# Moving a router's transposes, logits and row split into the last batch of the layer before it, and merging two blocks of an MoE layer

## The chip, the cores and the metric

The kernel runs on one core of one Trainium2 chip. The metric is device time in microseconds, the median of several executions. The core has five engines with instruction queues of their own: TensorE (PE; its weight loads are listed apart as PEld), VectorE (DVE), ScalarE (ACT), GpSimd (POOL) and SyncE (SP, which only issues transfers here). They meet by semaphores. TensorE's clock has two levels, 1.2 and 2.4 GHz, and the profile gives the granted share of the full one.

## The reference

One decoder layer on x of 32 batches x 112 rows x 256 columns, in float32. Three parts, each followed by a residual and a layer norm.

1. Self part: a linear attention with 16 heads and a feed-forward with gelu.
2. Cross attention: 16 heads of 64 over a context of 375 rows per batch. Per batch: normalise x and the context, q, k and v projections, softmax, values, output projection, then `x = layernorm(x + out)`.
3. A mixture of 8 experts, two per row, with 17 places (CAP) per expert and batch:

```
probs = softmax(x @ Wr + br);  topk_p, topk_e = top_k(probs, 2)
pos   = place of each row in its expert's queue, within the batch (cumulative count)
keep  = pos < 17
buf   = rows of x scattered to (expert, batch, pos)      # dispatch
y     = relu(buf @ W1 + b1) @ W2 + b2                    # per expert
out   = sum over the two choices of y[its place] * p * keep
x     = layernorm(x + out)
```

## The kernel before, in words

x stays in SBUF as `x_sb` (112 x 32 x 256, float32) through all three layers. Products that need accuracy are done in three float16 products of high and low halves (`split_product`, L62 to L64). Every stage is a block: each engine runs its own program, and all engines meet at the end of a block.

**Layer 2, the cross attention (L758 to L1439).** One batch is 16 steps (heads) s. In step s of batch b TensorE does, in this order: `turn_scores` (three transposes of the softmax's row block, L1016), one piece of the q, k or v projection of batch b+1 (L62 to L64), in even steps the scores of heads s+4 and s+5 (`scores`, L1007) and the values of heads s-2 and s-1 (`values`, L1032), and in step 3 the output projection of the batch before (`out_rows`). ScalarE does the exp of head s+2 (L1122), then the high half of the turned block (`turned_high`, L1128), then the high half of the piece. VectorE does the low halves, the reciprocal of the sum (L1236) and the masked maximum of head s+4 (`mask_max`, L1231). GpSimd normalises head s+2 (L1393) and prepares batch b+2. The scores of the next two heads wait until both maxima of the last two are taken. In the last batch, b = 31, there is no next batch: the pieces are gone and only turn, scores, values and the output projections are left. Its output rows are ready with the layer norm of batch 31 (`norm_out`, L1262). The projections' results go through three PSUM banks `pb` in turn. TensorE's program for the 32 batches is written out; on ScalarE, VectorE, GpSimd and SyncE batches 0, 1, 30 and 31 are written out, and 2 to 29 are a hardware loop of 14 turns over two batches.

**Route (L1503 to L1678).** After layer 2's block: for 8 groups of four batches, VectorE copies x to `xs` (L1631), TensorE turns it (8 float32 transposes, L1586), ScalarE copies the turned block to `xt` (L1604) and writes x's high half `x_hi` (L1606), TensorE multiplies it with the 256 x 8 router weights (8 float32 matmuls with 8 moving columns, L1577), VectorE adds the bias (L1621) and writes x's low half (L1627). `x_hi` and `x_lo` lie in `y_t`, which the experts fill later. Then the choice of two experts: 17 dependent VectorE operations on 112 x 256 (L1656 to L1678), with one exp on ScalarE and one counting matmul on TensorE. The split of the first expert's weights `w1` (high on ScalarE L1487, low on VectorE L1492) lies within route; the low half of `w2` comes first in the experts' block.

**Dispatch (L1681 to L1748).** A block of its own: per group, VectorE builds `gather` (0/1 matrix of 112 x 136 per batch, L1726), TensorE multiplies x_hi and x_lo with it (4 matmuls a batch into 4 + 4 banks, L1745), ScalarE copies the high result to `buf_hi` (L1711), VectorE the low result to `buf_lo` (L1721).

**Experts and combine.** The experts' block begins when dispatch has ended, and TensorE's first matmul there waits for `w1`'s low half.

Of the kernel before, what the change touches and what calls it, by code (L numbers as in the profile page):

```python
# [20 lines left out]
P = 128  # L21
# [5 lines left out]
KD = D // P  # L27
# [39 lines left out]
def decoder_kernel(nc, a, out):  # L67
    root = ExitStack()
    with root:
# [17 lines left out]
        layer2(nc, a, x_sb, ident, half_neg, passed, sb_in, psum_in, sem)  # L87
        layer3(nc, a, out, x_sb, ident, half_neg, passed, sb_in, psum_in, sem)
# [669 lines left out]
def layer2(nc, a, x_sb, ident, half_neg, passed, sb_in, psum_in, sem):  # L758
# [6 lines left out]
    with stack:  # L765
# [6 lines left out]
        stage = [sb(f"b_stage{i}", [P, WCOLS], F32) for i in range(NST)]  # L772
# [34 lines left out]
        o_hi, o_lo = (sb(f"b_o_{n}", [P, KI, T], F16) for n in ("hi", "lo"))  # L807
        z = sb("b_z", [T, D], F32)
# [25 lines left out]
        PRE = (turns(0) + [("P", 0, s) for s in range(PREP_AT)] + turns(1) + [("P", 0, s) for s in range(PREP_AT, NCH)])  # L834

        def body_uses(b):

            uses = []
            for s in range(H):
                if not is_last(b):  # L840
                    uses.append(("P", s))
                if s == W_AT and not is_first(b):
                    uses.append(("W", 0))
                if has_prep(b):
                    uses += [(kind, at.index(s)) for kind, at in (("X", X_AT), ("C", C_AT)) if s in at]
            if is_last(b):
                uses.append(("W", 1))
            return uses

        def is_first(b):  # L850
            return isinstance(b, int) and b == 0

        def is_last(b):
            return isinstance(b, int) and b == B - 1

        def has_prep(b):
            return not isinstance(b, int) or b + 2 < B

        PER = len(body_uses(None))
        assert PER % NPB == 0  # L860

        def use_in(b, item):

            less = 0 if is_first(b) else PER - len(body_uses(0))
            if is_last(b):
                less += PER - len(body_uses(B - 2))
            return b, len(PRE) - less + body_uses(b).index(item)

        def use_piece(n, s):
            return (0, PRE.index(("P", 0, s))) if is_first(n) else use_in(n - 1, ("P", s))  # L870

        def use_turn(n, kind, k):
            return (0, PRE.index((kind, n, k))) if isinstance(n, int) and n < 2 else use_in(n - 2, (kind, k))

        def use_out(b):
            return use_in(b, ("W", 1)) if is_last(b) else use_in(b + 1, ("W", 0))

        def ready(use):
            return use[0] * PER + use[1] + 1

        def freed(use):
            return use[0] * (PER // NPB) + use[1] // NPB + 1

        def bank(use):
            return pb[use[1] % NPB]

        def free_of(use):
            return pb_free[use[1] % NPB]

        w_loaded = [sem(f"b_w_loaded{i}") for i in range(NST)]  # L890
        w_hi_done, w_lo_done, vec_loaded = sem("b_w_hi_done"), sem("b_w_lo_done"), sem("b_vec_loaded")
        ctx_loaded = [sem(f"b_ctx_loaded{i}") for i in range(2)]
# [18 lines left out]
        def x_row(b):  # L911
            return x_sb[:, bass.ds(b, 1), :].rearrange("p a d -> p (a d)")

        def batches(eng, body):

            body(0, 0)
            body(1, 1)
            with eng.Fori(1, B // 2 - 1) as i:
# [8 lines left out]
        def _(sp):  # L927
            def load(n, par):
                settle(sp, passed, (xc_done, n - 1))
                sp.dma_start(ctx[:, par, :, :], a["ctx_1024"][bass.ds(n, 1), :, :].rearrange(  # L930
                    "a (p t) d -> p (a t) d", t=JT)).then_inc(ctx_loaded[par], 16)
                settle(sp, passed, (mask_done, n - 1))
                sp.dma_start(mask8[:, par, :], a["mask_BxS2_bf1"][bass.ds(n, 1), :].rearrange(
                    "a s -> (a s)").partition_broadcast(T)).then_inc(mask_loaded[par], 16)
# [5 lines left out]
            for i, src in enumerate(weights.values()):  # L940
                at_least(sp, w_lo_done, i - NST + 1)
                sp.dma_start(stage[i % NST][:, :].rearrange("p (k n) -> p k n", n=src.shape[2]), src).then_inc(w_loaded[i % NST], 16)
                if i == 0:
                    load(1, 1)
            with sp.Fori(1, B // 2) as i:
                for par in range(2):
                    load(2 * i + par, par)

        @block.tensor
        def _(pe):  # L950
            def claim(use):
                at_least(pe, pb_free[use[1] % NPB], freed(use) - 1)
                return bank(use)
# [37 lines left out]
            def written(n, *pieces):  # L991

                last = {}
                for s in sorted(PIECES.index(piece) for piece in pieces):
                    use = use_piece(n, s)
                    last[use[1] % NPB] = use
# [49 lines left out]

            def body(b, par):
                for s in range(H):
                    turn_scores(b, s)
                    if not is_last(b):  # L1050
                        piece(b + 1, 1 - par, s)
                    if s % 2 == 0 and s + AHEAD < H:
# [30 lines left out]
            for b in range(B):  # L1083
                body(b, b % 2)
# [4 lines left out]
        def _(act):  # L1089
# [28 lines left out]

            def softmax_exp(b, h):
# [17 lines left out]
            def split_high(name):  # L1137
                i = list(weights).index(name)
                act.wait_ge(w_loaded[i % NST], 16 * (i // NST + 1))
                act.activation(hi[name][:, :], stage[i % NST][:, :], ACT.Identity, scale=WSCALE).then_inc(w_hi_done, 1)  # L1140

            def body(b, par):
                for s in range(H):
# [9 lines left out]
                    if not is_last(b):  # L1153
                        piece_high(b + 1, 1 - par, s)
                    if s == SPLIT_O_AT and is_first(b):
# [24 lines left out]
            batches(act, body)  # L1180
# [3 lines left out]
        def _(dve):  # L1184
            def prep_stats(n, par, tiles):
                dve.wait_ge(ctx_loaded[par], 16 * (half_of(n) + 1))
# [20 lines left out]
            def piece_low(n, par, s):  # L1207
# [15 lines left out]
                ins.then_inc(pb_free[use[1] % NPB], 1)  # L1223

            def mask_max(b, par, h):

                waits = [(s_ready, H * b + h + 1), (p_exp, H * b + h - 1)]
                if h == 0:
# [3 lines left out]
                                         ALU.add, ALU.min, neg_max[:, h % 4:h % 4 + 1]).then_inc(s_masked, 1)  # L1232

# [30 lines left out]
            def split_low(name):  # L1264
                i = list(weights).index(name)
                dve.wait_ge(w_hi_done, i + 1)
                dve.scalar_tensor_tensor(lo[name][:, :], stage[i % NST][:, :], WSCALE, hi[name][:, :], ALU.mult,  # L1267
                                         ALU.subtract).then_inc(w_lo_done, 1)

            def body(b, par):  # L1270
                for s in range(H):
# [6 lines left out]
                    elif s == 0 and not is_first(b):  # L1278
                        piece_low(b, par, NCH - 1)
                    turned_low(b, s)  # L1280
# [25 lines left out]
            def half_of(n):  # L1306

                return n // 2 if isinstance(n, int) else halves[0]

            halves = [None]  # L1310
# [18 lines left out]
            body(0, 0)  # L1329
            body(1, 1)  # L1330
            with dve.Fori(1, B // 2 - 1) as i:
                halves[0] = i + 1
                for par in range(2):
                    body(2 * i + par, par)
            body(B - 2, 0)
            body(B - 1, 1)
# [6 lines left out]
        def _(pool):  # L1343
            def mask(n, par):
                settle(pool, passed, (mask_loaded[par], 16 * (half_of(n) + 1)),
# [32 lines left out]
            def split_ctx(n, par, k):  # L1378
                use = use_turn(n, "C", k)
                settle(pool, passed, (pb_free[use[1] % NPB], freed(use)))  # L1380
# [14 lines left out]

            def body(b, par):
                for s in range(H):
                    if s + 2 < H:
                        normalise(b, s + 2)
                    elif not is_last(b):  # L1400
                        normalise(b + 1, s + 2 - H)
                    if s == 0 and not is_last(b):
# [13 lines left out]
            def half_of(n):  # L1416
                return n // 2 if isinstance(n, int) else halves[par_of[0]]

            halves, par_of = [None, None], [0]
# [10 lines left out]
            body(0, 0)  # L1430
            body(1, 1)
            with pool.Fori(1, B // 2 - 1) as i:
                halves[0], halves[1] = i + 1, i
                for par in range(2):
                    par_of[0] = 1 - par
# [653 lines left out]
```

## Time and profile before

| | us |
|---|---|
| median of 3 runs | 2368.42 (2366.4 to 2376.06) |
| the profiled execution: its own time | 2368.95 |
| the profiled execution: span of its instructions | 2367.0 |
| TensorE busy | 2215.9 (94%) |
| VectorE busy | 1552.4 (66%) |
| ScalarE busy | 1385.2 (59%) |
| GpSimd busy | 744.0 (31%) |

TensorE's mean granted clock is 0.964. The page also cuts the span into 40 equal slices and gives busy shares in tenths; this is TensorE's row and the row of its clock:

```profile
PE   5999999999996599999999999999999999779998
PEclk8999999999998799999999999999999999659999
```

A slice is 59.2 us. Slices 13 and 14 hold the change from layer 1 to layer 2; slices 35 and 36 (2012 to 2130 us) hold the last batch of layer 2, route and dispatch. The last four slices are experts and combine.

### The profile page before, as it was taken

Reading aid. Unit: us, or ns where it says so; the run is one execution under the profiler, and the core shown is the slowest. Engines: PE = TensorE matmul, PEld = TensorE weight load, DVE = VectorE, ACT = ScalarE, POOL = GpSimd, SP = SyncE. Lnnn points to the kernel's source line nnn. Section 1 sums busy time; section 2 is a strip of 40 time slices with the busy share of each in tenths; the row PEclk is TensorE's granted clock in tenths of the full one; section 3 lists DMA queues with packets and bytes.
Section 4 is the critical chain, followed back from the end, with each engine's and each line's share of the span. In section 5 each row is a group of like instructions: output and inputs, shape, how many; then the busy total and the mean of one; then the engine's idle time right before and its main releaser. Section 6 shows DMA issues by size and latency. Waiting matters only on the chain. (4 is left out here: it accounts for less than half of the span.)

```text
span 2367.0 us, 60858 instructions
## 1 busy us (share of the span) xinstructions
PE 2215.9 (94%) x20706; PEld 1659.8 (70%) x20706; DVE 1552.4 (66%) x4402; ACT 1385.2 (59%) x3136; POOL 744.0 (31%) x1303
## 2 busy tenths in 40 slices
PE   5999999999996599999999999999999999779998
PEld 4776876876875367776767677777767676668886
DVE  4545545545544478777777777787777777466657
ACT  5556446446441467677676767676776767444444
POOL 1121221211211344444454544444444544100003
PEclk8999999999998799999999999999999999659999
DMA  5100000000000300000000000000000000212302
GB/s 137 36 2 1 0 0 0 0 0 0 0 1 1 100 11 14 15 9 15 9 15 10 15 9 15 12 13 15 9 15 9 15 2 2 73 22 87 106 1 63
DMA packets 45672, 50.94 MB, mean 22 GB/s; under 512 B 19120, under 2 KB 37664, under 8 KB 45504
## 3 DMA queue, kind: packets, MB, share of 16 engines
q1 hardware_dynamic: 45504, 48.45, 6.9%
q8 instruction: 136, 2.23, 0.4%
q14 instruction: 32, 0.26, 0.0%
HBM read 44.78 MB, written 3.67 MB: 20 GB/s over the span
## 5 line engine op out<-in xcount | busy, mean ns | idle before, releaser
L1393 POOL TENSOR_SCALAR p_norm<-p,p_rec 112x375 f32<-112x375 f32 x512 | 303.2, 593 | 638.2 <-DVE p_rec L1236 575.1
L1240 DVE TENSOR_TENSOR pt_lo<-b_t,pt_hi 125x336 f16<-125x336 f32 x512 | 258.0, 504 | 149.0 <-ACT pt_hi L1128 143.9
L1231 DVE CUSTOM_DVE_ANT_0 s_neg<-b_s,mask_bias 112x375 f32<-112x375 f32 x512 | 274.8, 537 | 94.0 <-PE b_s L1007 89.3
L1128 ACT ACTIVATE pt_hi<-b_t 125x336 f16<-125x336 f32 x512 | 227.3, 444 | 145.1 <-PE b_t L1016 141.3
L1122 ACT ACTIVATE p<-s_neg,neg_max 112x375 f32<-112x375 f32 x512 | 308.1, 602 | 1.3 <-DVE neg_max L1231 1.3
L1016 PE MATMUL b_t<-ident,p_norm 112*125 112x112 f32 x1536 | 274.6, 289 | 10.7 <-POOL p_norm L1393 5.4
L1016 PEld LDWEIGHTS b_t<-ident,p_norm 112*125 112x125 f32 x1536 | 216.1, 191 | 51.8 <-POOL p_norm L1393 28.9
L646 POOL TENSOR_SCALAR_AFFINE_SELECT sm<-sm 112x448 f32<-112x448 f32 x128 | 71.5, 581 | 433.1 <-ACT sm L430 433.1
L1116 ACT ACTIVATE v_hi<-b_pb 125x512 f16<-125x512 f32 x192 | 114.8, 598 | 111.3 <-PE b_pb L64 111.1
L62 PE MATMUL b_pb<-cn_hi,b_wk_hi 128*128 128x375 f16 x512 | 165.9, 324 | 1.9 <-DVE b_wk_lo L1267 1.9
L64 PE MATMUL b_pb<-cn_hi,b_wk_lo 128*128 128x375 f16 x512 | 165.1, 322 | 0.0
L63 PE MATMUL b_pb<-cn_lo,b_wk_hi 128*128 128x375 f16 x512 | 164.9, 322 | 0.0
L1113 ACT ACTIVATE k_hi<-b_pb 128x375 f16<-128x375 f32 x256 | 124.2, 485 | 61.3 <-PE b_pb L64 56.7
L430 ACT ACTIVATE sm<-a_s 112x448 f32<-112x448 f32 x128 | 62.5, 540 | 163.2 <-PE a_s L299 163.2
L62 PE MATMUL b_pb<-b_wv_hi,cn_hi 128*125 128x512 f16 x384 | 147.6, 384 | 5.3 <-issue 3.8
L64 PE MATMUL b_pb<-b_wv_hi,cn_lo 128*125 128x512 f16 x384 | 147.2, 383 | 0.0
L63 PE MATMUL b_pb<-b_wv_lo,cn_hi 128*125 128x512 f16 x384 | 147.0, 383 | 0.0
L1221 DVE SCALAR_TENSOR_TENSOR v_lo<-b_pb,v_hi 125x512 f16<-125x512 f32 x192 | 131.0, 682 | 18.2 <-ACT v_hi L1116 18.2
L1032 PE MATMUL b_o<-pt_hi,v_hi 125*64 125x112 f16 x1536 | 139.0, 223 | 1.8 <-DVE pt_lo L1240 1.8
L1216 DVE SCALAR_TENSOR_TENSOR k_lo<-b_pb,k_hi 128x375 f16<-128x375 f32 x256 | 138.3, 541 | 2.0 <-ACT k_hi L1113 2.0
L1032 PEld LDWEIGHTS b_o<-pt_hi,v_hi 125*64 125x64 f16 x1536 | 87.2, 110 | 73.0 <-issue 43.5
L1032 PE MATMUL b_o<-pt_lo,v_hi 125*64 125x112 f16 x1536 | 133.0, 215 | 0.0
(246 smaller groups left out, 6460.4 us busy)
## 6 DMA issues: line engine op xcount, KB each, us to landing
w_raw<-in_L_ffn_W_dram SPq DMA_DIRECT2D x16, 1024.0 KB, 7.4
ctx<-in_ctx_dram SPq DMA_DIRECT2D x32, 375.0 KB
out_dram<-c_z SPq DMA_DIRECT2D x8, 448.0 KB, 3.2
x_sb<-in_x_dram SPq DMA_DIRECT2D x1, 3136.0 KB, 19.1
ff<-in_L_attn_w_dram SPq DMA_DIRECT2D x2, 1024.0 KB, 7.1
b_stage<-in_L_xattn_Wkv_dram SPq DMA_DIRECT2D x2, 1024.0 KB, 10.0
mask<-in_mask_BxS_bf_dram SPq DMA_DIRECT2D x32, 41.0 KB, 2.6
a_raw<-in_L_attn_wq_dram SPq DMA_DIRECT2D x1, 1024.0 KB, 5.0
```

The source lines that it names most:

```text
L62: pe.matmul(out, lh, rh, start=first, stop=False)
L63: pe.matmul(out, lh, rl, start=False, stop=False)
L64: return pe.matmul(out, ll, rh, start=False, stop=last)
L1016: mm = pe.transpose(t_ps[h % 2][0:JP, t * T:(t + 1) * T], p_norm[:, h % 4, t * JP:(t + 1) * JP], ident[0:T, 0:T])
L1032: mm = pe.matmul(o_ps[DH * r:DH * (r + 1), c:c + T], v2[:, par, t, (h + r) * DH:(h + r + 1) * DH], pt[:, (h + r) % 4, keys], start=(t == 0 ...
L1122: act.activation(p32[:, h % 4, :], s_neg[:, h % 2, :], ACT.Exp, bias=neg_max[:, h % 4:h % 4 + 1], scale=-1.0, accum_out=p_sum[:, h % 4:h % ...
L1128: act.activation(pt_hi[:, h % 4, :], t_ps[h % 2][0:JP, 0:JT * T], ACT.Identity).then_inc(pt_hi_done, 1)
L1216: ins = dve.scalar_tensor_tensor(k2_lo[:, par, j, 0:S2], ps[:, 0:S2], UNSCALE, k2_hi[:, par, j, 0:S2], ALU.mult, ALU.subtract)
L1221: ins = dve.scalar_tensor_tensor(v2_lo[:, par, t, cols], ps[0:JP, :], UNSCALE, v2_hi[:, par, t, cols], ALU.mult, ALU.subtract)
L1231: dve.tensor_tensor_reduce(s_neg[:, h % 2, :], s_ps[h % 2][0:T, 0:S2], mask_bias[:, par, :], -1.0, 3.4e38, ALU.add, ALU.min, neg_max[:, h ...
L1240: dve.tensor_tensor(pt_lo[:, h % 4, :], t_ps[h % 2][0:JP, 0:JT * T], pt_hi[:, h % 4, :], ALU.subtract).then_inc(pt_lo_done, 1)
L1393: pool.tensor_scalar(p_norm[:, h % 4, :], p32[:, h % 4, :], p_rec[:, h % 4:h % 4 + 1], 0.0, ALU.mult, ALU.add).then_inc(p_norm_done, 1)
```

## The change

- Layer 2's last batch takes the router's work for the 31 batches that are finished by then, two batches a step. In step s TensorE first does the logits of step s-1's two batches (`route_logits`, 4 float32 matmuls), then four transposes straight from `x_sb` (`route_turn`); ScalarE copies the turned block (`xr`, 128 x 448) and writes `x_hi` for two batches (`route_columns`); VectorE adds the bias two steps later (`route_bias`, 112 x 16); GpSimd writes `x_lo` for two batches (`split_rows`, 112 x 512). Turned blocks and logits use the three `pb` banks.
- The two router transfers (`wr`, `br`) are issued within layer 2, behind its context loads.
- ScalarE, VectorE, GpSimd and SyncE no longer loop in layer 2: all 32 batches are written out.
- `y_t` is allocated for the whole kernel, and layer 2's three staging tiles for weights lie in it.
- Route and dispatch are one block. In it only batch 31 is turned, multiplied and split (low half on GpSimd). Both high halves of the first expert's weights follow the exp on ScalarE. Dispatch is written out, with three banks for each half in place of four, and each batch waits for its own bank; ScalarE takes the low result of every fourth batch besides all high ones. The low half of `w1` is the last VectorE operation of the block.

```
+            def route_turn(s):
+                pe.wait_ge(x_done, routed(s)[-1] + 1)
+                ps = claim(use_number["RT", s, 0])
+                for i, b in enumerate(routed(s)):
+                    for k in range(KD):
+                        c = (i * KD + k) * T
+                        mm = pe.transpose(ps[:, c:c + T], x_sb[:, b, k * P:(k + 1) * P], ident[0:T, 0:T])
+                mm.then_inc(pb_ready, 1)
+            def route_logits(s):
+                turned = use_number["RT", s, 0]
+                pe.wait_ge(free_of(turned), freed(turned))
+                pe.wait_ge(router_loaded, 32)
+                ps = claim(use_number["RL", s, 0])
+                for i, b in enumerate(routed(s)):
+                    for k in range(KD):
+                        c = (i * KD + k) * T
+                        mm = pe.matmul(ps[0:T, i * E:(i + 1) * E], xr[:, s % 2, c:c + T], wr[:, k, :], start=(k == 0), stop=(k == KD - 1))
+                mm.then_inc(pb_ready, 1)
             def body(b, par):                          # TensorE
                 for s in range(H):
                     turn_scores(b, s)
                     if not is_last(b):
                         piece(b + 1, 1 - par, s)
+                    else:
+                        if s > 0:
+                            route_logits(s - 1)
+                        route_turn(s)
...
+            def route_columns(s):                      # ScalarE, after turned_high(b, s)
+                act.activation(xr[:, s % 2, 0:n], bank(use)[:, 0:n], ACT.Identity).then_inc(free_of(use), 1)
+                act.activation(x_hi[:, rows, :], x_sb[:, rows, :], ACT.Identity).then_inc(x_hi_done, 1)
+            def split_rows(s):                         # GpSimd, after normalise(b, s + 3)
+                pool.tensor_tensor(x_lo[:, rows, :], x_sb[:, rows, :], x_hi[:, rows, :], ALU.subtract).then_inc(x_lo_done, 1)
...
-            body(0, 0)
-            body(1, 1)
-            with dve.Fori(1, B // 2 - 1) as i:
-                halves[0] = i + 1
-                for par in range(2):
-                    body(2 * i + par, par)
-            body(B - 2, 0)
-            body(B - 1, 1)
+            batches(body)                              # for b in range(B): body(b, b % 2)
+            for s in range(H - 2, H):
+                route_bias(s)
...
+            for b in range(B):                         # TensorE, dispatch
+                if b % G4 == 0:
+                    pe.wait_ge(gather_done, b // G4 + 1)
+                if b == LAST:
+                    pe.wait_ge(x_lo_done, 1)
+                if b >= NB:                            # NB = 3
+                    pe.wait_ge(hi_done, b - NB + 1)
+                    pe.wait_ge(*taken(b - NB))
...
+            for g in range(NG):                        # VectorE, dispatch
+                (gather of group g)
+                if g > 0:
+                    take(g - 1)                        # the three of four batches with b % 4 != 3
+            take(NG - 1)
+            weights_low(dve, 0, 0, 0)
```

## Rows read from the trace of the kernel before

**Rows 1.** Windows: PE, PEld, DVE, ACT, POOL busy us (instructions), granted clock, DMA, GB/s.
```profile
1900.00:2000.00 100.00, 98.52 (x1073) 71.47 (x1071) 76.46 (x245) 68.31 (x180) 42.53 (x76) 1.00 0.01 2
2019.70:2031.00 11.30, 6.86 (x96) 5.13 (x96) 8.06 (x30) 7.34 (x21) 4.31 (x8) 1.00 0.00 0
2031.00:2040.40 9.40, 7.63 (x76) 5.99 (x73) 4.00 (x13) 3.66 (x11) 2.37 (x4) 0.51 0.01 3
2053.00:2085.00 32.00, 32.00 (x176) 32.00 (x175) 16.30 (x22) 17.05 (x25) 0.00 (x0) 0.50 0.57 133
2305.00:2322.00 17.00, 16.86 (x113) 13.95 (x112) 13.32 (x42) 10.92 (x24) 7.10 (x17) 1.00 0.10 29
```

**Rows 2.** VectorE's timeline, layer 2's end to experts: start us, us, instruction, idle before.
```profile
2050.51 0.41 DVE L1262 TENSOR_SCALAR x_sb<-b_z,z_mom,z_rstd 112x256 f32<-112x256 f32 x1 [1.14 <-POOL z_rstd L1389]
...
2088.42 0.42 DVE L1656 TENSOR_REDUCE r_max<-logits 112x32 f32<-112x256 f32 x1
...
2098.70 1.36 DVE L1726 TENSOR_TENSOR gather<-place,slot_id 112x544 f16<-112x544 f32 x2 [0.32 <-PEq L1510]
...
2123.06 2.29 DVE L1492 SCALAR_TENSOR_TENSOR e_w_lo<-w_raw,e_w_hi 128x2048 f16<-128x2048 f32 x1 [0.33 <-PEq L1685]
```

**Rows 3.** TensorE's timeline in the last batch of layer 2.
```profile
2019.29 0.48 PE L1016 MATMUL b_t<-ident,p_norm 112*125 112x112 f32 x3
...
2023.20 0.37 PE L1007 MATMUL b_s<-k_hi,q_hi 64*112 64x375 f16 x2 [0.87 <-DVE neg_max L1231]
...
2023.81 0.24 PE L1032 MATMUL b_o<-pt_hi,v_hi 125*64 125x112 f16 x2
...
2024.37 0.91 PE L1016 MATMUL b_t<-ident,p_norm 112*125 112x112 f32 x6
2026.65 0.37 PE L1007 MATMUL b_s<-k_hi,q_hi 64*112 64x375 f16 x2 [1.37 <-DVE neg_max L1231]
...
2034.30 0.30 PE L1032 MATMUL b_o<-pt_hi,v_hi 125*64 125x112 f16 x2 [0.45 <-DVE pt_lo L1240]
...
2035.28 1.82 PE L1016 MATMUL b_t<-ident,p_norm 112*125 112x112 f32 x6
```

**Rows 4.** TensorE's timeline in route: logits and turns, four batches each.
```profile
2055.75 3.02 PE L1577 MATMUL r_logit<-wr,buf_hi 128*112 128x8 f32 x16
2058.62 1.74 PE L1586 MATMUL r_turn<-ident,buf_hi 112*128 112x112 f32 x8
2060.15 3.02 PE L1577 MATMUL r_logit<-wr,buf_hi 128*112 128x8 f32 x16
```

**Rows 5.** Groups of ScalarE and GpSimd operations: busy us, mean ns, idle before.
```profile
L1606 ACT ACTIVATE y_t<-x_sb x4 | 4.2, 1057 | 0.0
L1604 ACT ACTIVATE buf_hi<-r_turn 128x448 f32<-128x448 f32 x16 | 7.8, 542 | 25.2 <-PE r_turn L1586 25.2
...
L1393 POOL TENSOR_SCALAR p_norm<-p,p_rec 112x375 f32<-112x375 f32 x512 | 303.2, 593 | 638.2 <-DVE p_rec L1236 575.1 <-PE b_t L1016 63.2
L1383 POOL TENSOR_TENSOR cn_lo<-cn,cn_hi 128x375 f16<-128x375 f32 x60 | 52.5, 875 | 5.2
```

**Rows 6.** ScalarE's timeline in the last batch: exp, then the turned block's high half.
```profile
2028.41 0.60 ACT L1122 ACTIVATE p<-s_neg,neg_max 112x375 f32<-112x375 f32 x1
...
2029.00 0.44 ACT L1128 ACTIVATE pt_hi<-b_t 125x336 f16<-125x336 f32 x1
```

**Rows 7.** VectorE's timeline: the layer norm's last step in batches 1, 2 and 3.
```profile
889.67 0.41 DVE L1262 TENSOR_SCALAR x_sb<-b_z,z_mom,z_rstd 112x256 f32<-112x256 f32 x1
...
927.99 0.41 DVE L1262 TENSOR_SCALAR x_sb<-b_z,z_mom,z_rstd 112x256 f32 x1
...
966.23 0.41 DVE L1262 TENSOR_SCALAR x_sb<-b_z,z_mom,z_rstd 112x256 f32 x1
```

**Rows 8.** Groups in dispatch: the copies of the low and the high result.
```profile
L1721 DVE CAST buf_lo<-d_lo 128x272 f32 x24 | 10.1, 440 | 4.0 <-PE d_lo L1745 3.8
...
L1711 ACT ACTIVATE buf_hi<-d_hi 128x272 f32 x24 | 9.8, 410 | 9.2 <-PE d_hi L1745 9.2
```

More of the change, by code:

```diff
@@ L859, in layer2 @@
[L859 to L867, printed above, removed]
+            return b + 2 < B
+        USES = turns(0) + [("P", 0, s) for s in range(PREP_AT)] + turns(1) + [("P", 0, s) for s in range(PREP_AT, NCH)]
+        for b in range(B):
+            USES += body_uses(b)
@@ L1179, in _ @@
                 softmax_exp(0, h)
-            batches(act, body)
+            batches(body)
             out_high(B - 1, 1)
@@ L1429, in _, with layer3 @@
                 normalise(0, h)
[L1430 to L1435, printed above, removed]
-                    body(2 * i + par, par)
-            body(B - 2, 0)
-            body(B - 1, 1)
+            batches(body)
+            split_rows(H - 1)
             residual_rstd(B - 1)
-def layer3(nc, a, out, x_sb, ident, half_neg, passed, sb_in, psum_in, sem):
+def layer3(nc, a, out, x_sb, ident, half_neg, passed, wr, br, logits, y_t, x_hi, x_lo, sb_in, psum_in, sem):
     stack = ExitStack()
@@ L1536, in is_first, with on_act, taken, rows_of @@
-        def is_first(g):
-            return isinstance(g, int) and g == 0
-        def is_last(g):
-            return isinstance(g, int) and g == NG - 1
+        def on_act(b):
+            return b % 4 == 3
+        def taken(b):
+            before = [i for i in range(b + 1) if on_act(i) == on_act(b)]
+            return (lo_done_act if on_act(b) else lo_done), len(before)
+        def rows_of(g):
+            return slice(G4 * g, G4 * (g + 1))
+        def slots_of(buf, b):
+            return buf[:, :, :, b * CAP:(b + 1) * CAP]
@@ L1596, in _ @@
                       start=True, stop=True).then_inc(count_ready, 1)
+            for b in range(B):
+                if b % G4 == 0:
[5 more added lines that the diff above has]
+                    pe.wait_ge(*taken(b - NB))
+                for src, ps, done in ((x_hi, hi_ps, hi_ready), (x_lo, lo_ps, lo_ready)):
+                    for k in range(KD):
+                        mm = pe.matmul(ps[b % NB][:, k * SLOTS:(k + 1) * SLOTS], src[:, b, k * P:(k + 1) * P], gather[:, b, :],
+                                       start=True, stop=True)
+                    mm.then_inc(done, 1)
@@ L1610, in _ @@
-            groups(act, body)
+            act.wait_ge(turn_ready, 1)
+            act.activation(xt[:, :], turn_ps[:, 0:KD * T], ACT.Identity).then_inc(xt_done, 1)
+            act.activation(x_hi[:, LAST, :], x_sb[:, LAST, :], ACT.Identity).then_inc(x_hi_done, 1)
             act.wait_ge(step, 2)
             act.activation(work["exp"][:, :, :], logits[:, :, :], ACT.Exp).then_inc(exp_done, 1)
-            weights_high(act, 0, 0, 0, 1)
+            for which in range(2):
+                weights_high(act, 0, 0, 0, which)
@@ L1640, in _ @@
-            groups(dve, body)
-            for par in range(2):
-                add_bias(NG - 2 + par, par)
-            dve.wait_ge(logit_done, NG)
+            dve.wait_ge(logit_ready, 1)
+            dve.tensor_tensor(logits[:, LAST, :], logit_ps, br[:, :], ALU.add).then_inc(logit_done, 1)
+            dve.wait_ge(logit_done, 1)
             dve.wait_ge(const_done, 2)
@@ new lines, in _ @@
+                                     count_ps, ALU.mult, ALU.add).then_inc(step, 1)
+            dve.wait_ge(step, 17)
+            def take(g):
+                for b in range(G4 * g, G4 * (g + 1)):
+                    if not on_act(b):
+                        dve.wait_ge(lo_ready, b + 1)
+                        dve.tensor_copy(slots_of(buf_lo, b), bank_slots(lo_ps, b)).then_inc(lo_done, 1)
+            for g in range(NG):
+                dve.tensor_tensor(gather[:, rows_of(g), :].rearrange("p b (e c) -> p (b e) c", c=CAP),
+                                  place[:, rows_of(g), :].rearrange("p b e -> p (b e)").unsqueeze(2).to_broadcast([T, G4 * E, CAP]),
```

301 lines of the change are left out of this document (114 added, 187 removed).

## The prediction, made before the changed kernel was run

> **What bounds the kernel now.** I read the 40 slices first: TensorE is nearly full everywhere but at the change of layers and in slices 35 and 36. Then windows of those. In the middle of layer 2 TensorE is busy 98.5 of 100 us at full clock [rows 1]: what other engines save there is worth nothing. In the last batch the pieces are gone and it is busy 6.9 of 11.3 us, waiting [rows 1]. Then, in route, it is busy for all of 32 us at granted clock 0.50, the 1.2 GHz level [rows 1]: there it sets the end again, with transposes and router matmuls only.
>
> The timelines give the chain. Batch 31's rows are ready with the operation that starts at 2050.51; the choice starts at 2088.42, the first `gather` at 2098.70, the experts at 2123.06 [rows 2]. So 37.9 us of route lie between the last rows and the choice, and 24.4 us between the first gather and the experts. Nothing else runs beside them.
>
> In the last batch the order is one cycle per two steps: scores at 2023.20, values at 2023.81, two turns at 2024.37, then TensorE waits 1.37 us for the masked maximum until the next scores at 2026.65 [rows 3]. The cycle is 3.45 us: scores 0.61, values 0.56, turns about 0.9, the rest is the way over ScalarE's high half and VectorE's low half and maximum.
>
> **Part 1, the head of the choice.** Removed from after the last batch: seven groups and three quarters of the eighth. What is left for batch 31: the block's start, 0.33 us [rows 2]; two transposes, at 0.19 each (1.53 us for eight, start to start [rows 4]); one copy of 224 columns, at most the 0.54 of 448 columns [rows 5]; two logit matmuls at 0.36 (2.87 us for eight [rows 4]) = 0.72; the bias, under the 0.42 of a choice operation on 112 x 256 [rows 2]; three hand-overs, 0.2 each by my estimate. Sum 0.33 + 0.38 + 0.4 + 0.72 + 0.2 + 0.6 = 2.6 after 2050.9, so the choice starts 3.1 us after the 2050.51 operation, not 37.9: **-34.8 us** (-33.5 to -35.5). Copy to `xs`, and VectorE's `x_lo`, go too; they were beside TensorE. The exp stays where it was. Both weight halves on ScalarE (2 x 1.9, VectorE's counterpart is 2.29 [rows 2]) come under the 10 us of the choice; the four expert loads that they need are now issued without the two router loads ahead of them on SP. The choice itself is the same 17 operations: 0.
>
> **Part 2, what the last batch pays.** Per step it gains four transposes, 0.77 at 1.2 GHz, and four logit matmuls, 1.43 [rows 4]: 2.2 us at the slow level, 1.1 at the full one, if the weight load follows the clock; no row shows a logit matmul at full clock, so 1.1 to 2.2 is the bound. TensorE's work per two steps is then:
> - full clock: 0.61 + 0.56 + 0.91 + 2.2 = 4.3;
> - half clock: twice the scores (1.2), values 0.98 as from 2034.30 to 2035.28, turns 1.6 to 1.8 [rows 3], 4.4 = 8.3.
>
> The 1.4 us of waiting in the cycle is filled by this. The other engines: ScalarE per step 0.59 from exp to the next [rows 6], about 0.35 for the high half, 0.44 to 0.54 for the turned block, 0.53 for `x_hi` (half of 1057 ns for twice the rows [rows 5]) = 1.95, or 3.9 per two steps. GpSimd: 0.59 plus `x_lo`; 875 ns for 375 columns gives 1.2 for 512 [rows 5], or 3.6. VectorE adds a small add. So TensorE bounds, with ScalarE close. The logits of step s wait for ScalarE's copy, which stands behind exp and high half; mostly TensorE has turn, scores or values to do meanwhile; I add 0.15. Pair: 4.45 at full clock, 8.3 at half. The last four steps have no scores: 3.9 and 7.
>
> Which clock? It decides the case. Before, the same steps ran at 1.00 until 2031 and at 0.51 after it [rows 1], though TensorE was only 60% busy in both. The dense output projection ended at 2019.29 [rows 3], right ahead of the full stretch. With the router's work the engine is busier, but with transposes and 8-column matmuls, and these alone had 0.50 for 32 us of unbroken work [rows 1]. On the other side combine holds 1.00 with transposes between larger float32 matmuls [rows 1]. I take half of the time at each level. From 2019.29 to the end of step 15 (about 2040.3) there are 12 steps: full 4 x 4.45 + 2 x 3.9 = 25.6, half 4 x 8.3 + 2 x 7 = 47.2, mean 36.4 against 21.0: +15.4. The first four steps hold four turns and three logit groups, 3.9 at full clock; the waits there absorb about two: +2, or +5 at half clock, I take +3.5. The tail (values, projection of batch 31 at half clock, norm) stays: the last router step adds up to 1.5, a full clock would give back 2.5. Sum **+18.9 us** (+4.5 all at full clock; all at half +5 + 26.2 + 1.5 = +32.7).
>
> The Trainium skill, TensorE: Matmul & The Clock Gate, Part 4 (PE-mode transpose), says that transposes don't count as busy work for the clock. Route's 0.50 agrees; combine's 1.00 neither proves nor refutes it, since real matmuls stand between. By the rule the whole last batch would fall to the half level, which is rival B.
>
> **Part 3, dispatch.** Before: from 2098.70 to 2123.06 less the block change of 0.33, 24.0 us for eight groups, 3.0 each [rows 2]. Now VectorE has 0.7 for the gather and three copies of at most 0.44 = 2.0; ScalarE five of at most 0.41 = 2.05 [rows 8]; TensorE four batches of matmuls, about 0.45 each at half clock (estimate: 4 x 136 columns at 1.2 GHz) = 1.8. With three banks each batch waits for the one three before: matmuls, hand-over, copy, hand-over is some 1.2 us, 0.4 a batch, inside the pace. I take 2.2 a group: 17.6, plus 0.8 to the first result and 0.5 for the last copy, 18.9. Then `w1`'s low half, 2.29 [rows 2], which before lay beside TensorE's logits and now stands alone on the path, since the experts wait for it; and 0.33 for the block. 21.5 against 24.4, and the block change at 2098.70 goes, 0.3: **-3.2 us**. Bounds: -6 (1.9 a group), or +2 (3.0 a group still, plus the 2.29).
>
> **Part 4, batches written out.** Batch 1 (written out) to 2 (loop) is 38.32 us from norm to norm, 2 to 3, both in the loop, 38.24 [rows 7], and TensorE was always written out. 0, within -1 and +2 us over 28 batches. The Trainium skill, Runtime: NRT & Kernel Launch (Instruction fetch mechanics), says that a taken branch breaks the prefetch of instructions, so that written-out code is the better. A turn of the loop costs nothing that rows 7 show, so by the trace this gives no gain here: the engines concerned wait for TensorE. The early router loads and the staging tiles in `y_t` change no order: 0.
>
> **Sum.** -34.8 + 18.9 - 3.2 = -19.1. From the profiled execution's own 2368.95 (0.5 above the median of 2368.42) that is 2349.9; against the median, 2349.3. I predict **2349**.
>
> **Rivals.**
> - **A, the clock holds.** The last batch costs 4.5: -34.8 + 4.5 - 3.2 = -33.5, 2335. For it: combine's 1.00, and that TensorE no longer waits. Against: 0.51 from 2031 on.
> - **B, the clock falls in the first steps and stays** but after the projection in step 3, whose effect saved one pair before (3.85 less): +28.9, total -19.1 + 10 = -9.1, 2359. For it: route's 0.50, and a part of the last batch that is thinner in real matmuls than before.
> - **C, slower.** The router's chain is served one piece after another: each logit group waits for the copy behind exp, high half and `x_hi` on ScalarE (about 1.9 us) while TensorE has nothing else ready, at half clock. Then a step is 4.15 + 1.9, a pair 12.1, and six pairs are 72.6 less 2.6 for missing scores = 70 against 21: +49; with +6.5 beside it, total +17.5, 2386. It decides from a pair of 8.75 us on average: the gains are 38.0, 6.5 of them spent beside the six pairs, and 31.5 over six pairs are 5.25 above the 3.5 of before. Against: the copies of step s are asked for a full turn, scores and values later.
> - **D, dispatch gains nothing** (+2 in place of -3.2), last batch as forecast: 2354.
>
> **Chances.** Forecast (mixed clock, 2342 to 2355) 0.43; A 0.22; B 0.22; C 0.06; D 0.07. A measurement of this kernel can tell 0.5%, 11.8 us, from no change: the borders are 2356.6 and 2380.3. The forecast lies within the faster side but for 0.02, A wholly, B for 0.07 of its 0.22, D for 0.05: faster 0.75; C is slower at 0.05; same 0.20. The range takes A's centre less a little and B's: 2332 to 2362.
>
> **What would show it.** The choice's first reduction about 3.1 us after the last `x_sb` norm. Ends of the last batch: its norm at 2069 (2055 in A, 2079 in B). Scores to scores in that batch: 4.4 or 8.3 us, next to a granted clock of 1.00 or 0.50. TensorE busy over 90% there. The first gather to the experts in 21 to 22 us, with 2.29 of `w1` alone at its end. Norm to norm still 38.3 in the middle. Wrong would be: a pair well over 8.3 us with TensorE idle, waits for the turned copy, or a changed period of the written-out batches.

## The result

The changed kernel takes 2351.3 us (median of 8 runs, 2341.5 to 2360.4) against 2373.7 for the kernel before beside it (8 runs): ratio 0.9908, 95% interval 0.9884 to 0.9932. That is 22 us, where 19 were forecast, and the time of 2351.3 stands beside a forecast of 2349.

The profiled execution has its own time 2344.2 and a span of 2342.5, 24.5 less than the span before. VectorE's timeline of the changed kernel, with the lines that answer to [rows 2]:

```profile
1959.47 0.41 DVE L1314 TENSOR_SCALAR x_sb<-b_z,z_mom,z_rstd 112x256 f32<-112x256 f32 x1
...
2068.74 0.41 DVE L1314 TENSOR_SCALAR x_sb<-b_z,z_mom,z_rstd 112x256 f32<-112x256 f32 x1 [1.12 <-POOL z_rstd L1433]
2071.48 0.17 DVE L1654 TENSOR_TENSOR logits<-r_small,br 112x8 f32<-112x8 f32 x1 [2.32 <-PE r_small L1615]
2071.68 0.42 DVE L1668 TENSOR_REDUCE r_max<-logits 112x32 f32<-112x256 f32 x1
...
2081.68 1.36 DVE L1701 TENSOR_TENSOR gather<-place,slot_id 112x544 f16<-112x544 f32 x2
2083.14 1.35 DVE L1698 CAST buf_lo<-d_lo 128x272 f16<-128x272 f32 x3
2084.40 0.72 DVE L1701 TENSOR_TENSOR gather<-place,slot_id 112x544 f16<-112x544 f32 x1
...
2087.89 0.71 DVE L1701 TENSOR_TENSOR gather<-place,slot_id 112x544 f16<-112x544 f32 x1
2088.53 1.13 DVE L1698 CAST buf_lo<-d_lo 128x272 f16<-128x272 f32 x3
2089.57 0.71 DVE L1701 TENSOR_TENSOR gather<-place,slot_id 112x544 f16<-112x544 f32 x1
...
2096.08 2.28 DVE L1527 SCALAR_TENSOR_TENSOR e_w_lo<-w_raw,e_w_hi 128x2048 f16<-128x2048 f32 x1
2098.68 2.29 DVE L1527 SCALAR_TENSOR_TENSOR e_w_lo<-w_raw,e_w_hi 128x2048 f16<-128x2048 f32 x1 [0.32 <-PEq L1544]
```

The first two lines are the layer norms of batches 28 and 31 (the norm of batch 28's rows runs within the steps of batch 29, and that of batch 31's rows behind all steps). In the kernel before they began at 1961.37 and 2050.51:

```profile
1961.37 0.41 DVE L1262 TENSOR_SCALAR x_sb<-b_z,z_mom,z_rstd 112x256 f32 x1
```

So the 24.5 us are made up as follows. Between these two norms, 37.48 us pass in both kernels until batch 29's norm; the difference of the second row lies in the steps that follow it.

| stretch | before | after | difference |
|---|---|---|---|
| start to batch 28's norm | 1961.4 | 1959.5 | -1.9 |
| batch 28's norm to batch 31's | 89.1 | 109.3 | +20.1 |
| batch 31's norm to the choice | 37.9 | 2.9 | -35.0 |
| choice to the first gather | 10.3 | 10.0 | -0.3 |
| first gather to the experts' first VectorE operation | 24.4 | 17.0 | -7.4 |
| experts and combine | 243.9 | 243.8 | -0.1 |

Windows of the changed kernel, columns as in [rows 1]: the first steps of the last batch, its middle, its end, then dispatch.

```profile
2006.70:2017.80 11.10, 10.75 (x126) 9.51 (x126) 6.35 (x25) 9.37 (x24) 6.33 (x8) 1.00 0.01 1
2017.80:2031.00 13.20, 12.40 (x127) 10.17 (x127) 5.44 (x23) 8.63 (x21) 7.64 (x10) 0.87 0.01 2
2031.00:2058.30 27.30, 27.26 (x187) 23.49 (x187) 8.38 (x32) 13.62 (x32) 12.58 (x14) 0.50 0.01 2
2081.70:2098.70 17.00, 12.44 (x129) 9.32 (x130) 16.31 (x34) 12.95 (x40) 0.00 (x0) 0.88 0.37 13
```

TensorE never waits in the third window and has the 1.2 GHz level. TensorE's timeline gives the router's share at both levels (L1069 logits, L1058 turns, L1021 the softmax's turns):

```profile
2009.17 0.86 PE L1069 MATMUL b_pb<-wr,xr 128*112 128x8 f32 x8
2009.89 0.58 PE L1058 MATMUL b_pb<-ident,x_sb 112*128 112x112 f32 x4
2010.31 0.49 PE L1021 MATMUL b_t<-ident,p_norm 112*125 112x112 f32 x3
2011.10 0.95 PE L1069 MATMUL b_pb<-wr,xr 128*112 128x8 f32 x8 [0.31 <-ACT xr L1154]
...
2033.64 1.53 PE L1069 MATMUL b_pb<-wr,xr 128*112 128x8 f32 x8
2035.02 0.99 PE L1058 MATMUL b_pb<-ident,x_sb 112*128 112x112 f32 x4
2035.80 0.83 PE L1021 MATMUL b_t<-ident,p_norm 112*125 112x112 f32 x3
```

Start to start, a step's logits are 0.72 us at full and 1.38 at half clock, its turns 0.42 and 0.78: a float32 logit matmul, with its weight load, follows the clock, which the forecast had left open (1.1 to 2.2 a step). TensorE waits for ScalarE's copy in 11 of the 16 steps, 4.4 us in all.

At half clock two steps take what the forecast had: 8.3 us with scores, from the values at 2031.89 to those at 2040.18, and 7.2 without them, from there to 2047.36 (forecast 8.3 and 7). At full clock they take 4.8, scores at 2007.58 to scores at 2012.42, where 4.45 were forecast.

```profile
2031.89 0.30 PE L1037 MATMUL b_o<-pt_hi,v_hi 125*64 125x112 f16 x2
...
2040.18 0.31 PE L1037 MATMUL b_o<-pt_hi,v_hi 125*64 125x112 f16 x2
```

### The profile page after: what moved, and what is told of

It is laid out like the page before. It is cut to its first block and busy times, and to the rows that moved or that the text cites. A ratio compares the mean times of both kernels' runs of the same rounds, so it can differ in the third digit from the quotient of the medians.

```text
span 2342.5 us, 57663 instructions
## 1 busy us (share of the span) xinstructions
PE 2203.3 (94%) x20706; PEld 1645.9 (70%) x20706; DVE 1530.9 (65%) x4387; ACT 1386.6 (59%) x3154; POOL 758.6 (32%) x1320
## 5 line engine op out<-in xcount | busy, mean ns | idle before, releaser
L1021 PE MATMUL b_t<-ident,p_norm 112*125 112x112 f32 x1536 | 275.5, 289 | 8.3 <-POOL p_norm L1437 2.4
L1021 PEld LDWEIGHTS b_t<-ident,p_norm 112*125 112x125 f32 x1536 | 216.7, 191 | 49.0 <-POOL p_norm L1437 26.1
## 6 DMA issues: line engine op xcount, KB each, us to landing
x_sb<-in_x_dram SPq DMA_DIRECT2D x1, 3136.0 KB, 19.1
```

Of the source, the lines that this page charges most:

```text
L1021: mm = pe.transpose(t_ps[h % 2][0:JP, t * T:(t + 1) * T], p_norm[:, h % 4, t * JP:(t + 1) * JP], ident[0:T, 0:T])
```

## The experiments

All ratios are to the kernel before in the same session. The changed kernel itself ran beside them in every session but that of `heat1`, `w1pool`, `written` and `dve4`. Because the point where the clock falls differs from run to run, and the start of layer 2 too (batch 0's norm is at 889.6 in the first profile and at 906.2 in another of the same kernel, with no change to layer 1), the profiles are compared by stretches: batch 28's norm to batch 31's, called the last stretch here, and first gather to experts. The expectations call the first of these norms batch 29's, since it runs within that batch's steps; the stretch is the same.

**The same kernel again, three times.**

> The changed kernel once more, to see how far its runs spread and why. Theory 1 (the last batch's cost is TensorE's router work times the granted clock, and the point where the clock falls is not the same in each run): the profiled run has its batch-31 norm anywhere from 2055 to 2076 us, the rest of the program within 1 us of the first profile, and the spread of the runs (2341 to 2360) lies in that batch. Rival (something else moves: layer 2's middle or the experts): norm to norm in the middle, or gather to end, differ by several us between the two profiles.

> The changed kernel on the same chip as the best version, for the comparison. A third profile of it: clock lost for 25 to 45 us of the last batch, batch 29's norm to batch 31's 105 to 118 us, all else within 1 us of the first two but for the start of layer 2.

> The changed kernel on the same chip as the best version. A fourth profile: batch 29's norm to batch 31's 105 to 118 us with the clock at 0.50 for 25 us or more of it; first gather to experts 17.0.

Measured: 2356.8 (0.9931 of before, 0.9903 to 0.9960), 2353.6 (0.9894, 0.9857 to 0.9932) and 2352.9 us (0.9898, 0.9861 to 0.9936). The last stretch was 117.0, 116.9 and 117.0 us, against 109.3 in the first profile. The batches around it in the second of the three:

```profile
1976.27 0.41 DVE L1314 TENSOR_SCALAR x_sb<-b_z,z_mom,z_rstd 112x256 f32<-112x256 f32 x1
...
2093.20 0.41 DVE L1314 TENSOR_SCALAR x_sb<-b_z,z_mom,z_rstd 112x256 f32<-112x256 f32 x1 [1.12 <-POOL z_rstd L1433]
```

and its windows over the last batch, where TensorE is busy in all of the 36 us at 0.50:

```profile
2023.30:2046.00 22.70, 21.86 (x195) 19.26 (x193) 9.66 (x38) 13.65 (x35) 9.78 (x12) 0.77 0.01 2
2046.00:2082.00 36.00, 35.96 (x244) 30.66 (x242) 10.72 (x42) 17.99 (x43) 16.77 (x20) 0.50 0.00 1
```

Two experiments further down, `w1pool` and `dve4`, change only what comes after layer 2, so their last stretches are samples of the same program, and `written` is one more of the program before:

| profile | batch 0's norm at | last stretch |
|---|---|---|
| changed kernel, first profile | 889.6 | 109.3 |
| rep | 888.0 | 117.0 |
| rep2 | 906.2 | 116.9 |
| rep3 | 885.4 | 117.0 |
| w1pool | 896.0 | 103.1 |
| dve4 | 898.3 | 109.3 |
| kernel before | 889.7 | 89.1 |
| written (layer 2 as before on TensorE) | 909.9 | 85.3 |

So the last batch pays 14.0, 20.1 (twice) or 27.8 us (three times) over the 89.1 of before, and that base moves too. What differs is when the clock falls. In rep, rep2 and rep3 it fell early, came back around the output projection of step 3 and fell again. In w1pool it held until 2045:

```profile
2006.00:2045.50 39.50, 36.91 (x422) 30.16 (x420) 23.96 (x86) 30.48 (x78) 21.61 (x29) 1.00 0.01 2
2045.50:2060.00 14.50, 14.02 (x113) 12.47 (x113) 2.93 (x11) 6.97 (x17) 7.38 (x8) 0.54 0.00 1
```

Theory 1 of the first expectation, that the spread of the runs lies in this batch, is wrong in part. rep took 2351.7 and rep2 2370.9 us with the same last stretch, and 18.2 of these 19.2 us had passed before batch 0's norm. Layer 1 moves with the clock too (0.90 against 0.96 in its first 200 us, 0.95 against 1.00 from 400 to 600).

**Logits exchanged for transposes** (shortened)**.**

```
-  four logit matmuls a step
+  for _ in range(5):
+      pe.transpose(ps[:, P:P + T], x_sb[:, b, 0:P], ident[0:T, 0:T])
+  mm = pe.matmul(ps[0:T, 0:n * E], xr[:, s % 2, 0:T], wr...[:, 0:n * E], start=True, stop=True)
```

> Leaves out three of each step's four logit matmuls (logits are wrong) and puts five float32 transposes in their place, about the same TensorE time (0.7 us a step at full clock). Theory 2 (transposes count as work for the clock like other matmuls): granted clock 1.00 through the last batch, two steps 4.3 us, batch 31's norm near 2053, kernel about 2330. Rival, the Trainium skill's rule that transposes do not count (TensorE: Matmul & The Clock Gate, Part 4): clock 0.50 from the middle of the batch as in the changed kernel, two steps near 8 us, norm near 2068.

```profile
2023.30:2060.00 36.70, 34.16 (x414) 29.20 (x413) 19.09 (x77) 30.69 (x77) 24.96 (x31) 1.00 0.01 2
```

This kernel leaves out three of four logit matmuls a step, so its logits are incomplete. The clock stays at 1.00 through the whole batch and to the end of its output projection. The last stretch is 93.2 us (1975.85 to 2069.02), 4.0 over before. By the ratio the kernel is at 0.9833 (0.9791 to 0.9876), clear of the changed kernel's 0.9931 (0.9903 to 0.9960) beside it. With transposes in place of logits, for about the same time of TensorE, the clock held in this profile; with four logit matmuls a step it was lost in all six profiles above. The Trainium skill (TensorE: Matmul & The Clock Gate, Part 4) says that transposes don't count as busy for the clock. The 0.50 that the expectation's rival drew from that rule did not come, so for this mixture the measurement decides; but scores and values stand between the transposes, and one profile does not refute the rule.

**Fewer logits, nothing instead.** The same diff without the five transposes; the logits are incomplete here too.

> Leaves out three of each step's four logit matmuls (logits are wrong), nothing in their place. Theory 1: TensorE's work per two steps falls by 1.1 us at full and 2.1 at half clock; ScalarE's 3.9 us becomes the bound where the clock is full; batch 31's norm at 2050 to 2058, 10 to 18 us before the changed kernel's. Rival (the batch is bound by the hand-over over ScalarE's copy): norm moves by less than 5 us.

```profile
2023.00:2048.00 25.00, 21.53 (x235) 17.16 (x233) 14.03 (x56) 20.33 (x52) 15.67 (x20) 0.93 0.01 2
2048.00:2066.00 18.00, 16.54 (x131) 13.40 (x129) 6.26 (x26) 12.13 (x29) 11.52 (x13) 0.51 0.01 1
```

The last stretch is 98.8 us: 18 less than in rep beside it, though only 4 less than in the best profile of the changed kernel's program. The runs are clearer: 0.9797 (0.9763 to 0.9831) against 0.9931 (0.9903 to 0.9960). So the router's work on TensorE is what the batch pays, and not the hand-over. But it is 5.6 us longer in this profile than with the transposes, though TensorE does less: the clock was lost in the last third. The two profiles entered layer 2 alike (batch 0's norm at 905.0 and 905.3). Over several runs the medians stand the other way (0.9797 against 0.9833) with intervals that overlap, so which of these two is faster is open.

**Dense work that nobody needs.**

```
                 ps = claim(use_number["RT", s, 0])
+                for _ in range(2):
+                    pe.matmul(ps[:, 0:512], hi["q"][:, 0:P], hi["k"][:, 0:512], start=True, stop=True)
                 for i, b in enumerate(routed(s)):
```

> Adds to every router turn in the last batch two dense float16 matmuls of 512 columns into the same bank (overwritten by the turns): 32 matmuls, 6.8 us of TensorE work at full clock, 13.7 at half; results unchanged. Theory 1 with a clock that is lost because router work is thin: the last batch runs at 1.00 throughout, two steps take 5.1 us instead of up to 8.3, batch 31's norm comes at about 2056 instead of 2069 and the kernel is 8 to 14 us faster although it does more (about 2337). Rival (the clock falls whatever TensorE is given, or the batch is bound by waits): norm at 2075 to 2082, kernel 7 to 14 us slower.

> One dense float16 matmul of 512 columns with each router turn of the last batch in place of two (16 of them, 3.4 us at full clock). If one is enough to hold the clock: 1.00 to the end of step 15, batch 29's norm to batch 31's in about 99 us (109.3 and 117.0 in the changed kernel's two profiles, 102.7 with two), 3 us less than with two. If it is not: the clock falls once in the batch, 103 to 112 us.

With two matmuls a step: 2343.7 us against 2356.8 for the changed kernel in the same session, ratios 0.9869 (0.9840 to 0.9897) and 0.9931 (0.9903 to 0.9960), whose intervals don't overlap. The last stretch is 102.7 us with 32 matmuls more in it:

```profile
2014.90:2060.00 45.10, 42.63 (x463) 34.59 (x463) 20.01 (x79) 31.62 (x77) 26.16 (x32) 1.00 0.01 2
```

With one a step the profile has 101.9 us and clock 0.96 in the window 2008 to 2060, and the ratio 0.9887 (0.9861 to 0.9913) is not apart from the changed kernel's in the other sessions. The rival, that the clock falls whatever TensorE is given, is out. How much the dense work gives rests on the runs and not on these profiles: w1pool, which entered layer 2 like them (896.0 against 896.9 and 895.5), has 103.1 us without any.

**GpSimd makes w1's low half** (`w1pool`)**.** Scaling and subtraction on GpSimd after the exp, VectorE's operation at the end of dispatch removed.

> The low half of the first expert's w1 is made by GpSimd (a scaling and a subtraction on 128 x 2048) beside the choice instead of by VectorE after the last copy. Theory 1: it stands alone on the path in the changed kernel, so the first gather to the experts' first VectorE operation falls from 17.0 to 14.7 us. Rival: GpSimd takes longer than choice and dispatch together (24 us), or slows VectorE's choice operations beside it (0.42 each before), and the gain is under 1 us.

VectorE's and GpSimd's timelines of this kernel:

```profile
2077.67 3.32 DVE L1691 TENSOR_TENSOR r_eq<-r_left,r_max 112x256 f32<-112x256 f32 x1
...
2084.63 3.32 DVE L1709 TENSOR_TENSOR gather<-place,slot_id 112x544 f16<-112x544 f32 x2
2088.04 1.35 DVE L1706 CAST buf_lo<-d_lo 128x272 f16<-128x272 f32 x3
...
2101.84 2.29 DVE L1527 SCALAR_TENSOR_TENSOR e_w_lo<-w_raw,e_w_hi 128x2048 f16<-128x2048 f32 x1 [0.77 <-PEq L1551]
```

```profile
2076.77 5.68 POOL L1532 TENSOR_SCALAR w_raw<-w_raw 128x2048 f32<-128x2048 f32 x1 [5.13 <-ACT e_w_hi L1522]
2082.54 4.20 POOL L1534 TENSOR_TENSOR e_w_lo<-w_raw,e_w_hi 128x2048 f16<-128x2048 f32 x1
```

Choice to gather is 12.9 us, not 10.0, and first gather to experts 17.2, where 14.7 were expected: what was saved was lost twice. One comparison took 3.32 us instead of 0.42, two gathers took 3.32 instead of 1.36, both while a long GpSimd operation ran; other VectorE operations beside the same work took their usual 0.42. This is one profile, and that GpSimd's work is the cause is inferred from the overlap. The ratio, 0.9921 (0.9887 to 0.9955), tells nothing. A miss.

**Only written out** (`written`)**.** The kernel before, with layer 2's batches and dispatch as plain `for` loops, all else as it was.

> The kernel before with layer 2's batches and dispatch written out, nothing else. Theory 1: norm to norm in the middle of layer 2 falls from 76.55 us for two batches to 76.40, as in the changed kernel, 2 us in all; dispatch (first gather to experts) falls from 24.4 to 20 us or less, since registers and not engines set its pace of 3.2 us a group. Rival: the pace of dispatch came from the order of copies and banks, and it stays at 23 to 24 us; the changed kernel's 1.68 us a group then comes from ScalarE's share and the waits per bank.

```profile
2113.56 1.36 DVE L1704 TENSOR_TENSOR gather<-place,slot_id 112x544 f16<-112x544 f32 x2 [0.31 <-PEq L1491]
2116.74 0.71 DVE L1704 TENSOR_TENSOR gather<-place,slot_id 112x544 f16<-112x544 f32 x1
2118.76 0.72 DVE L1704 TENSOR_TENSOR gather<-place,slot_id 112x544 f16<-112x544 f32 x1
...
2131.10 2.29 DVE L1473 SCALAR_TENSOR_TENSOR e_w_lo<-w_raw,e_w_hi 128x2048 f16<-128x2048 f32 x1 [0.32 <-PEq L1666]
```

First gather to experts is 17.5 us where it was 24.4, with four banks, all low copies on VectorE and the old order of waits: 2.03 us a group instead of some 3. Norm to norm in layer 2's middle is 38.21 for each batch, where it was 38.31 and 38.24 in turn. The ratio is 0.9953 (0.9931 to 0.9974): about 11 us. Dispatch accounts for 6.8 of them and layer 2's middle for some 1.5; the last stretch may have a part by chance of the clock (85.3 us in this profile).

**VectorE takes all low copies of dispatch.**

> The changed kernel with all low results of dispatch copied by VectorE, none by ScalarE. If VectorE bounds dispatch, each group takes its four copies at 0.35 and the gather at 0.64: 2.05 us instead of 1.68, and first gather to experts 20 instead of 17.0 us. If TensorE or the banks bound it: 17 to 17.5 us.

```profile
2093.67 0.71 DVE L1701 TENSOR_TENSOR gather<-place,slot_id 112x544 f16<-112x544 f32 x1
2095.70 0.72 DVE L1701 TENSOR_TENSOR gather<-place,slot_id 112x544 f16<-112x544 f32 x1
...
2110.03 2.29 DVE L1527 SCALAR_TENSOR_TENSOR e_w_lo<-w_raw,e_w_hi 128x2048 f16<-128x2048 f32 x1 [0.32 <-PEq L1544]
```

2.03 us a group, and 19.5 us from first gather (2090.50) to experts: VectorE bounds dispatch, and ScalarE's fourth batch is worth 2.5 us. The pace is that of `written`, which has four banks and the old waits, so the three banks and the wait per bank gave the pace nothing. (Ratio 0.9916, 0.9883 to 0.9950, not apart from the changed kernel.)

**Two tries for a better version.** Both put half of w1's low half (`e_w_lo` in two parts of 1024 columns) into VectorE's wait for the counting matmul. The first has no dense matmul in steps 0 to 3, one in 4 to 11, two in 12 to 15; the second two in every step.

> The changed kernel with 16 dense matmuls of 512 columns put where the last batch is thin (none in steps 0 to 3, one a step in 4 to 11, two in 12 to 15), and with half of w1's low half (1.15 us) in the 1.35 us in which VectorE waits for the counting matmul. Theory 1: clock 1.00 from step 4 to 15, batch 29's norm to batch 31's 97 to 102 us, first gather to experts 15.9 instead of 17.0, choice unchanged at 10.0; 10 to 14 us under the changed kernel beside it. Rival (the clock still falls at some point, or the half of w1 delays the choice): norm to norm over 103, or choice over 10.3, and under 8 us gained.

> Two dense matmuls of 512 columns in every one of the 16 steps, and half of w1's low half in VectorE's wait for the counting matmul. Theory 1 (two in every step hold the clock from any phase; the thinner doses of the last two tries did not): clock 1.00 to the end of step 15, batch 29's norm to batch 31's 100 to 104 us, first gather to experts 16.0; 8 to 13 us under the changed kernel beside it, and a spread of runs of 12 us or less. Rival (the clock is lost from some phases even so): norm to norm over 106 us and no clear gain over the changed kernel.

The first missed: 2345.0 us, 0.9890 (0.9848 to 0.9932), not apart from the changed kernel's 0.9894 beside it; its profile had the clock at 0.50 again and a last stretch of 114.6:

```profile
2006.60:2024.00 17.40, 16.57 (x189) 14.32 (x188) 9.47 (x38) 12.98 (x33) 9.54 (x12) 1.00 0.01 2
2024.00:2038.00 14.00, 13.10 (x114) 10.11 (x113) 5.29 (x21) 8.65 (x22) 7.15 (x11) 0.75 0.00 1
2038.00:2065.00 27.00, 26.50 (x174) 21.20 (x174) 5.59 (x22) 10.63 (x26) 10.51 (x12) 0.50 0.00 1
```

The second takes 2337.9 us (5 runs, 2333.8 to 2351.0), 0.9846 of before (0.9813 to 0.9879), against 2352.9 and 0.9898 (0.9861 to 0.9936) for the changed kernel beside it. Medians are 15 us apart; the intervals overlap a little, so better than the changed kernel is likely, not shown. Its last stretch is 104.3 us, with clock 0.96 from 2006 to 2052: the clock was lost once and came back, so two dense matmuls a step don't hold it every time. The spread of the runs, 17 us, is also over the 12 that were expected. The half of w1 does what it was to do in both; the second's VectorE:

```profile
2074.59 0.42 DVE L1693 TENSOR_TENSOR r_left<-r_one,r_two 112x256 f32<-112x256 f32 x1
2075.05 1.22 DVE L1530 SCALAR_TENSOR_TENSOR e_w_lo<-w_raw,e_w_hi 128x1024 f16<-128x1024 f32 x1
2076.30 0.42 DVE L1696 SCALAR_TENSOR_TENSOR place<-r_left,r_small 112x256 f32<-112x256 f32 x1
...
2092.69 2.29 DVE L1530 SCALAR_TENSOR_TENSOR e_w_lo<-w_raw,e_w_hi 128x2048 f16<-128x2048 f32 x1 [0.32 <-PEq L1549]
```

First gather (2076.76) to experts is 15.9 us instead of 17.0, choice to gather still 9.9.

## Why the prediction was right, and where not

**The head of the choice** (forecast -34.8): -35.0. Right in size; from norm to choice 2.9 us against 3.1.

**What the last batch pays** (forecast +18.9, +4.5 at full clock, +28.9 in rival B with the clock back after step 3): +20.1 in the first profile; over the six profiles of the same program +14.0, +20.1 twice and +27.8 three times; and +4.0 where the clock held because transposes stood in for logits. The mechanism stands: TensorE's router work fills the waits and is then paid in proportion to the clock, at 8.3 us for two steps at half clock as forecast. That the first profile came within 1.2 us of the forecast's mean of the two levels is luck, since the point where the clock falls moves the cost by 14 us from one execution to the next. Three of the six profiles are mixed as forecast and three are at B's end. B had two reasons. The run with transposes speaks against the first, that transposes are what loses the clock; the second, a batch thinner in real matmuls, is left. With two dense matmuls a step added, the clock was at 1.00 to 2060 us in one profile and was lost once in the other. Why the logit matmuls lose it is not shown.

Two slips of the working: the window before that began at 2031.00 has TensorE busy in 7.63 of 9.40 us, 81% and not 60% [rows 1]; and the +4.5 does not follow from its own terms, 25.6 - 21.0 + 2 - 2.5 = 4.1. Neither moves the forecast.

**Dispatch** (forecast -3.2, bounds -6 to +2): -7.6, outside the bounds, the step that was mis-sized. The forecast's -3.2 takes in the block change at the first gather, so -7.4 and -0.3 of the table belong to it. I took a copy at its busy 0.44 and the pace at 2.2 us a group. Three copies in a row take 1.04 us up to the next gather's start (2088.53 to 2089.57), 0.35 each; with 0.64 from the gather's start to the first copy (2087.89 to 2088.53) that is 1.68 a group. So the busy time of one was the wrong measure for a row of operations, and 0.52 too much in each of eight groups are 4.2 us, nearly all of the miss.

What the gain is due to is another question, and here I put none of the old pace down to the hardware loop, though the old dispatch had gaps on every engine. The written-out kernel shows that writing out alone gives 6.8 us. On top of it ScalarE's share gives 2.5, and w1's low half takes back 2.3 (2.28 busy, nothing beside it; the block change behind it is in both kernels). That makes 17.3 from 17.5, and 17.0 were measured; 0.3 is left for banks, waits and the merged block together.

**Batches written out** (forecast 0): -1.9 from the start to batch 28's norm, and 1.2 to 1.7 less than before from batch 0's norm to batch 28's in the three other profiles. The bound was -1. I compared one batch that begins written out with loop batches and overlooked that loop batches alternate between 38.31 and 38.24, where written-out ones take 38.20 to 38.23:

```profile
927.85 0.41 DVE L1314 TENSOR_SCALAR x_sb<-b_z,z_mom,z_rstd 112x256 f32<-112x256 f32 x1
966.05 0.41 DVE L1314 TENSOR_SCALAR x_sb<-b_z,z_mom,z_rstd 112x256 f32<-112x256 f32 x1
```

38.20 here, 38.24 in [rows 7]. The Trainium skill (Runtime: NRT & Kernel Launch, Instruction fetch mechanics) says that a taken branch breaks the prefetch of instructions when its target is not in the pages at hand. That points the right way in both stages; these runs don't tell a fetch from register work in the loop.

**The sum**: -19.1 forecast, -24.5 in the first profile, some -17 with the longest of the last stretches (24.5 - (27.8 - 20.1) = 16.8), -22.4 between the medians. Two errors partly cancel: the last batch is dearer than forecast in five of six profiles, dispatch cheaper by 4.4.

**Rivals.** A (the clock holds) did not occur in the six profiles; B (it falls early) occurred in three of them; C (a chain over ScalarE's copy) is out, since TensorE is busy 27.26 of 27.30 us and waits 4.4 us for that copy in all; D (dispatch gains nothing) is out.

## What to carry to other kernels

Work moved into the shadow of an engine's waits is free only up to these waits, and on TensorE its price is set by the clock that the stretch keeps: look at both levels in rows and price both, and take several profiles before a cause is named, since one program's last stretch was anything from 103 to 117 us. Count small float32 matmuls by their number and not by their columns: one of 8 columns took 0.18 us where a transpose of 112 columns took 0.105. Where they must stand in a thin stretch, dense work beside them can shorten it. A stage whose engines all have gaps inside a hardware loop should be written out first, before its banks and shares are rearranged. Time a row of short operations from start to start, not by the busy time of one.

## What the runs showed of the hardware

- A float32 matmul of 8 columns, with its weight load, follows TensorE's clock: 0.72 us for the four of two batches at full, 1.38 at half clock.
- The clock was 1.00 over a window of 36.7 us in the run that has five more transposes per step.
- TensorE can be busy in 27.26 of 27.30 us and still have the 1.2 GHz level, here with transposes, 8-column logits, scores and values.
- TensorE got more work and the kernel became faster: 13 us less beside the same chip's run of the kernel without it, with 32 matmuls of 512 columns added.
- The same program's last stretch took 103.1, 109.3 or 117.0 us, by when the clock fell.
- Beside long GpSimd operations single VectorE operations took some 2 to 3 us longer (3.32 instead of 0.42), and GpSimd's own scaling of 2048 columns took 5.68 us. Which VectorE operation is held and why not its neighbours stays open.
